# An attention layer in front of a mixture of experts: the softmax sums of a head move to two buffers, and three engines share the work on them differently

## The reference, cut to what matters

```
x = x + attention(layernorm(x))          # 1024 tokens, 384 channels, 12 heads of 32
t = x + moe(layernorm(x))                # 8 experts, top 2, hidden width 1536

attention, for each head:
  s   = (q * scale) @ k.T + rel_h + rel_w      # 1024 x 1024
  p   = softmax(s)                             # over the keys
  out = p @ v                                  # 1024 x 32
  then out @ w_proj + b_proj
```

## Time and profile before

| what | value |
|---|---|
| median of 3 runs | 608.98 us (608.33 to 609.45) |
| the profiled execution | 610.03 us, of which the span from first to last instruction is 608.2 us |
| TensorE busy | 584.4 us, 96% of the span |
| VectorE, ScalarE, GpSimd busy | 387.2, 297.9, 195.3 us |
| mean granted TensorE clock | 0.994 of full speed |
| attention, heads 0 to 11 | about 82 to 283 us of the span |
| experts | about 320 to 608 us |

### The profile page before, as it was taken

How to read it: one execution, slowest core, us unless ns; L and a number is a source line. 1 busy time by engine, 2 the same in 40 slices (tenths; PEclk the granted TensorE clock), 3 DMA queues, 4 the chain that set the end, 5 groups by cost and what they waited for, 6 DMA issues and landing times.

```text
span 608.2 us, 11363 instructions
## 1 busy us (share of the span) xinstructions
PE 584.4 (96%) x4409; PEld 504.5 (83%) x4409; DVE 387.2 (64%) x644; ACT 297.9 (49%) x411; POOL 195.3 (32%) x114
## 2 busy tenths in 40 slices
PE   2998999999999999999999999999999999999996
PEld 1886786667776667767987999999999999999994
DVE  6656777777777677732978974555476545377525
ACT  3555424555555555554546445444545454455523
POOL 0400048989888888898000000000000000000000
PEclk9999999999999999999979999999999999999999
DMA  9046045333334444103231534444442444442302
GB/s 272 9 87 130 3 107 110 78 72 68 66 66 87 86 87 87 41 2 105 79 117 57 178 128 139 137 150 149 155 157 80 156 156 156 156 156 85 111 1 103
DMA packets 37414, 63.39 MB, mean 104 GB/s; under 512 B 3864, under 2 KB 32894, under 8 KB 37246
## 3 DMA queue, kind: packets, MB, share of 16 engines
q1 hardware_dynamic: 37374, 62.83, 36.6%
HBM read 44.16 MB, written 1.57 MB: 75 GB/s over the span
## 4 chain that ended last, share of the span: by engine, by line
PE 90%; DVE 5%; ACT 2%; DMA 1%; issue 1%; SPq 1%; DVEq 0%
PE ps L782 21%; PE ps L798 21%; PE ps L557 14%; PE ps L566 9%; PE ps L466 8%; PE ps L544 7%; DVE rhalf L1146 2%; PE ps L716 1%; PE ps L496 1%; PE ps L451 1%; DMA onehot<-c_onehot 1%; PE ps L753 1%; PE ps L728 1%; PE ps L809 1%; PE ps L590 1%
## 5 line engine op out<-in xcount | busy, mean ns | idle before, releaser
L1146 DVE TENSOR_REDUCE rhalf<-ps 128x1 f32<-128x512 f32 x192 | 131.4, 691 | 33.5 <-PE ps L544 32.4
L400 POOL TENSOR_TENSOR acc<-acc,prob 128x1024 f32<-128x1024 f32 x58 | 139.7, 2408 | 9.3 <-ACT prob L938 4.6
L938 ACT ACTIVATE prob<-ps 128x1024 f32<-128x1024 f32 x96 | 98.1, 1028 | 80.5 <-PE ps L557 80.3
L557 PE MATMUL ps<-qst,kst 128*128 128x512 f32 x384 | 115.6, 397 | 0.9 <-ACT prob L938 0.9
L427 POOL CAST dpc<-dpt 120x1024 fp32r<-120x1024 f32 (+1 forms) x3 | 3.1, 1039 | 275.1 <-PE ps L818 216.6
L782 PE MATMUL ps<-xeh,wih 128*128 128x320 f32 x288 | 89.6, 311 | 1.0 <-ACT xeh L1002 1.0
L798 PE MATMUL ps<-hh,woh 128*128 128x320 f32 x288 | 89.2, 310 | 0.0
L798 PE MATMUL ps<-hh,wol 128*128 128x320 f32 x288 | 89.0, 309 | 0.0
L782 PE MATMUL ps<-xeh,wil 128*128 128x320 f32 x288 | 89.0, 309 | 0.0
L798 PE MATMUL ps<-hl,woh 128*128 128x320 f32 x288 | 89.0, 309 | 0.0
L782 PE MATMUL ps<-xel,wih 128*128 128x320 f32 x288 | 89.0, 309 | 0.0
(11 more groups left out here) (159 smaller groups left out, 876.1 us busy)
## 6 DMA issues: line engine op xcount, KB each, us to landing
raw_i<-in_L_ffn_wi SPq DMA_DIRECT2D x32, 576.0 KB, 5.1
raw_o<-in_L_ffn_wo SPq DMA_DIRECT2D x32, 576.0 KB, 4.1
xs<-in_x SPq DMA_DIRECT2D x8, 384.0 KB, 4.8
qst<-qh SPq DMA_DIRECT2D x12, 256.0 KB, 3.1
qst<-relh SPq DMA_DIRECT2D x12, 256.0 KB, 3.8
qst<-relw SPq DMA_DIRECT2D x12, 256.0 KB, 4.4
kst<-kp SPq DMA_DIRECT2D x12, 256.0 KB, 5.0
qst<-ql SPq DMA_DIRECT2D x12, 128.0 KB, 3.1
```

Of the source, the lines that this page charges most:

```text
L400: nc.gpsimd.tensor_tensor(acc[:, :], acc[:, :], prob[:, slot_of(j, t), :], ALU.add).then_inc(sum_add, 1)
L557: last = mm(bank(2 * (t % 2) + half), kst[b][:, part, t * P:(t + 1) * P], qst[b][:, part, half * BANK:(half + 1) * BANK], start=part == 0, ...
L938: run(prob[:, slot_of(j, t), :], ps[:, 2 * (t % 2) * BANK:2 * (t % 2 + 1) * BANK], ACT.Exp).then_inc(exp_done, 1)
L1146: ve.tensor_reduce(rhalf[:, p // 2, p % 2:p % 2 + 1], bank(4 + p % 2), AX_X, ALU.max).then_inc(max_red, 1)
```

## The change

- There are two buffers for the denominator. GpSimd adds tiles 0 to 5 into `acc` as before, and its last addition, of tile 6, writes the new buffer `total`. It waits there (and no longer at the first addition) until TensorE has read the head before. The first addition of a head waits only until GpSimd's own last addition of the head before is done.
- VectorE adds tile 7 to `total` (`add_last`), between pieces 5 and 6 of the next head's maxima. TensorE's product of ones with tile 7 is gone in heads 0 to 10, and its product with the sum now waits for VectorE (`acc_whole`). The last head stays as it was, but for the order of one wait.
- ScalarE copies the head's values into `vh`, after the exponential of tile 5 of the head before.
- VectorE's loop over heads becomes two heads written out and two passes of three heads.
- `bpj` and `tri` share the place of two `vh` buffers and are loaded after the last scores, ahead of the rows of `x`. GpSimd's bias addition and the router's count wait for both.

Core of the diff:

```
@@ gpsimd
-            def head_values(h, b):
-                wait(pool, pv_mm, PAIRS_T * (h - 2))
-                nc.gpsimd.tensor_copy(vh[b][:, :, :], vt[:, :, bass.ts(h, HD)]).then_inc(vh_ready, 1)
             def add_probs(h, j, added=ADDED):
                 pool.wait_ge(exp_done, NT * h + 2)
-                wait(pool, pv_mm, PAIRS_T * h)
+                wait(pool, sum_add, (ADDED - 1) * h)
                 nc.gpsimd.tensor_tensor(acc[:, :], prob[:, slot_of(j, 0), :], prob[:, slot_of(j, 1), :], ALU.add).then_inc(sum_add, 1)
                 for t in range(2, added):
                     pool.wait_ge(exp_done, NT * h + t + 1)
                     pool.wait_ge(sum_add, (ADDED - 1) * h + t - 1)
-                    nc.gpsimd.tensor_tensor(acc[:, :], acc[:, :], prob[:, slot_of(j, t), :], ALU.add).then_inc(sum_add, 1)
+                    if t == added - 1:
+                        wait(pool, pv_mm, PAIRS_T * h)
+                    nc.gpsimd.tensor_tensor((total if t == added - 1 else acc)[:, :], acc[:, :],
+                                            prob[:, slot_of(j, t), :], ALU.add).then_inc(sum_add, 1)
+            pool.wait_ge(late_in, 32)
             for t in range(NT):
                 pool.wait_ge(x_in[t // XT], 32)
@@ tensor, values
                 if i == PAIRS_T - 1:
-                    quarters(slice(Q4, 2 * Q4), ones[:, 0:HD], prob[:, slot_of(b, NT - 1), :], False, False)
-                    pe.wait_ge(sum_add, (ADDED - 1) * (h + 1) - (ADDED - LAST_ADDED) * h_last)
-                    last = quarters(slice(Q4, 2 * Q4), ones[:, 0:HD], acc[:, :], False, True)
+                    if not h_last:
+                        pe.wait_ge(acc_whole, h + 1)
+                    last = quarters(slice(Q4, 2 * Q4), ones[:, 0:HD], total[:, :], False, True)
@@ scalar
+            def head_values(h, b):
+                wait(act, pv_mm, PAIRS_T * (h - 2))
+                run(vh[b][:, :, :], vt[:, :, bass.ts(h, HD)], ACT.Copy).then_inc(vh_ready, 1)
+                    if t == 5:
+                        head_values(h + 1, (j + 1) % 3)
@@ vector
+            def add_last(h, j):
+                dve.wait_ge(sum_add, (ADDED - 1) * (h + 1))
+                dve.wait_ge(exp_done, NT * (h + 1))
+                ve.tensor_tensor(total[:, :], total[:, :], prob[:, slot_of(j, NT - 1), :], ALU.add).then_inc(acc_whole, 1)
+            def head(h, j, first=False, early=False, more=True):
                 for p in range(0 if first else NEXT, 2 * NT):
+                    if p == NEXT + 1 and not first:
+                        add_last(h - 1, (j + 2) % 3)
@@ sync
             sp.wait_ge(s_mm, 8 * NH)
+            sp.wait_ge(pv_mm, PAIRS_T * (NH - 1))
+            sp.dma_start(bpj[:, :], b_proj.partition_broadcast(P)).then_inc(late_in, 16)
+            sp.dma_start(tri[:, :], tri_c).then_inc(late_in, 16)
```

More of the change, by code:

```diff
@@ L76, in metaformer_layer @@
     wrt = new("wrt", [P, DC, E])
+    s0 = at[0]
     stats = new("stats", [P, NT, 6])
@@ L83, in metaformer_layer @@
     gsc = new("gsc", [PS, NT])
+    at[0] = max(at[0], s0 + 4 * P)
     base = at[0]
@@ L117, in metaformer_layer @@
     wph = place("wph", [P, DC, D], F32R, q0 + 8 * T)
-    o4 = room(4 * 2 * BANK)
+    o4 = room(4 * BANK + 4 * T)
+    total = place("total", [P, T], F32, o4 + 4 * BANK)
     osb = place("osb", [P, BANK], F32, o4)
+    l0 = at[0]
     vh = [new(f"vh{b}", [P, NT, HD]) for b in range(3)]
-    mneg = place("mneg", [NT, P], F32R, o4 + 7 * BANK)
+    tri, bpj = place("tri", [P, P], F32, l0), place("bpj", [P, D], F32, l0 + 4 * P)
+    mneg = place("mneg", [NT, P], F32R, s0)
     rl = new("rl", [P, 2, NT // 2])
@@ L161, in metaformer_layer @@
     lmax, lsum, lrec = (new(n, [P, NT]) for n in ("lmax", "lsum", "lrec"))
-    assert at[0] <= end and max(top, end) <= nc.sbuf_usable_end
+    assert at[0] <= end <= l0 and max(top, end) <= nc.sbuf_usable_end
     ctx = ExitStack()
@@ L932, in free_slot @@
                     wait(act, sum_add, (ADDED - 1) * then + max(1, was))
+                else:
+                    wait(act, acc_whole, then + 1)
             def exps(h, j, between):
@@ L948, in attn_high, with between, at_tile @@
                     run(ath[:, c, half * BANK:(half + 1) * BANK], bank(4 + half), ACT.Copy).then_inc(turn_act, 1)
-            exps(0, 0, lambda t: None)
+            def between(h, j):
+                def at_tile(t):
+                    if t == 1:
+                        copy_output(h - 1)
+                    if t == 5:
+                        head_values(h + 1, (j + 1) % 3)
+                return at_tile
+            act.wait_ge(v_dve, NT)
+            head_values(0, 0)
+            exps(0, 0, lambda t: head_values(1, 1) if t == 5 else None)
             with act.Fori(0, (NH - 3) // 3) as i:
                 for j in range(1, 4):
-                    exps(3 * i + j, j % 3, lambda t: copy_output(3 * i + j - 1) if t == 1 else None)
-            exps(NH - 2, (NH - 2) % 3, lambda t: copy_output(NH - 3) if t == 1 else None)
+                    exps(3 * i + j, j % 3, between(3 * i + j, j % 3))
+            exps(NH - 2, (NH - 2) % 3, between(NH - 2, (NH - 2) % 3))
             def last_between(t):
@@ L1168, in _ @@
             NEXT = 5
-            def head(h, first=False, early=False, more=True):
+            def add_last(h, j):
[3 more added lines that the diff above has]
+            def head(h, j, first=False, early=False, more=True):
                 for p in range(0 if first else NEXT, 2 * NT):
+                    if p == NEXT + 1 and not first:
+                        add_last(h - 1, (j + 2) % 3)
                     if p == 8 and not first and not early:
@@ L1193, in _ @@
                     negate_max(0)
-            head(0, first=True)
-            head(1, early=True)
-            with dve.Fori(2, NH - 2) as h:
-                head(h)
-            head(NH - 2, more=False)
+            head(0, 0, first=True)
+            head(1, 1, early=True)
+            head(2, 2)
+            head(3, 0)
+            with dve.Fori(0, (NH - 6) // 3) as i:
+                for j in range(4, 7):
+                    head(3 * i + j, j % 3)
+            head(NH - 2, (NH - 2) % 3, more=False)
+            add_last(NH - 2, (NH - 2) % 3)
             def attn_low(c):
```

17 lines of the change are left out of this document (8 added, 9 removed).

## The result

The changed kernel took 620.07 us, the median of 4 runs (617.78 to 628.21), against 608.65 us for the kernel before on the same chip (608.08 to 609.45). The ratio is 1.0168, with a 95% interval of 1.0145 to 1.0191. So the changed kernel is slower by about 10 to 11 us. The forecast was 622.3, in a range from 617 to 634. The profiled execution took 620.59 us, with a span of 618.3 against 608.2.

The account below looks back on a forecast made before the run. TensorE, busy 96% of the span, was the bound. Head 0 (+0.35), nine heads (7.1) and head 10 bring +9.8 on 608.98: 618.8; none to three lost races at 2.3 each put the middle at 622.3, range 617 to 634.

Parts of the forecast that it names:

- The ring: TensorE's denominator, tile 2's scores and exponential, GpSimd's five additions, VectorE's addition: no slack, 0.79 us more a head.
- P: Start of a head's timeline: TensorE's load of weights for piece 8, at 153.38 in head 4 before the change.
- The step to piece 8: On TensorE, from the load for the sum to the load for piece 8: 0.76 us, next P at P + 17.45.
- Head 10: GpSimd copies `wph` first (1.14 us), so VectorE starts 1.1 us later and adds 1.22; TensorE then at +9.8 us.
- The stall at piece 10: TensorE waits some 0.6 us at piece 10 for piece 8's late reduction; no cost by itself, but delays next tile 1.
- The race: VectorE's addition against GpSimd's next first one, both after GpSimd's last addition; margins about 0.05 us; none to three lost: 0.55.
- The price of a lost race: If GpSimd goes first, VectorE starts 2.3 us later and a head takes 19.8 us.
- GpSimd first in all ten heads: Rival: GpSimd beats VectorE in all ten heads, 642 us; four or more heads, 628 to 642, had chance 0.30.
- Who holds the port: VectorE and GpSimd share ports under an exclusive lock: whoever starts first runs whole; sharing would cost under 1.2 us a head.
- ScalarE's copies at nothing: ScalarE's copy of the values, put in 3.25 us of idle time ahead of tile 6: free, at most 1 us a head.
- The late transfers at nothing: Two more transfer issues and 256 KB ahead of the rows of `x`: hidden, some 2 us of cover at the tightest.
- queue behind the wait: Rival: reductions queued behind VectorE's wait make the next maximum row late, one more us a head, 629; chance 0.07.

Follow-up runs that it names:

- the kernel that lost seven: Changed kernel with VectorE's addition placed later, behind the reductions of pieces 5 to 7 and the division; VectorE was second in seven heads; 642.79 us.
- the kernel with half an addition: Changed kernel with VectorE adding only 512 of the 1024 columns of tile 7, the other half left out of the denominators; 622.74 us.

## Why the prediction was right, point by point

- *The ring.* Right, and shown from three sides: with VectorE's addition out all but 1.1 us of the cost is gone (610.05), with half of it the heads are 0.55 us shorter, and with tile 2's scores ahead of the wait TensorE no longer waits for `total`. The sizes were P + 15.33, 16.65 and 16.69 for event, sum and load; the trace has 15.38, 16.64 and 16.69 in a head written out, and 15.40, 16.75 and 16.80 in VectorE's loop, where its addition starts 0.12 us after the event and not 0.10.
- *The step to piece 8* was put at 0.76 us behind the load for `total` and took 0.60 in every head. With the later loads in the loop this makes 17.29 to 17.43 where 17.45 was forecast, 6.5 us over nine heads instead of 7.1.
- *Head 10*: 2.3 forecast, 2.04 measured. VectorE's addition there is recorded at 276.82 with 2.13 us, behind GpSimd's copy of `wph` (276.72, 1.15).
- *The stall at piece 10*: 0.6 forecast, 0.55 measured at 124.16 and up to 0.67 in the loop, and no cost by itself, as said: where it was taken away and VectorE still went first, heads took as long.
- *The race.* The margins were forecast at about 0.05 us; by the starts of the rows they are 0.00 to 0.01 in four heads of the loop and 0.04 to 0.24 in the others. The forecast's 622.3 counted one or two lost races. The profiled run lost none, and its time, 620.59, is the sum for none (610.03 and 9.8 are 619.8) and 0.8 more. So the middle of the forecast was high by its races, some 3.5 us, and its sum low by what came before the first scores (1.17 us) and by 0.4 for the table load, less what the heads and the end took less. Whether the run of 628.21 lost some can't be told, since it has no trace; its granted clock of 0.985 would fit, between the 0.995 of the profiled run and the 0.972 to 0.977 of the kernel that lost seven.
- *Luck.* The path and its lengths were right by their working, but that the time came within the range hung on four heads decided by 0.01 us or less. Had these been lost, at 2.2 us or more each, the time would have been about 629 or more (an estimate), and the forecast gave 628 to 642 a chance of 0.30.
- *The price of a lost race* at 2.3 us was right for the race alone and left the clock out. The single lost race in the kernel with half an addition cost 2.2 us (TensorE waited 2.63 us, and its clock stayed full), and the first one of the later-addition kernel 2.3 (19.54 against 17.28). Where TensorE's clock fell as well, such heads took 20.6 to 22.0, 3.2 to 4.6 us over 17.4. The rival "GpSimd first in all ten heads" was put at 642 and its kernel took 662.76; with seven lost it was 642.79.
- *Who holds the port.* The rows said that the two instructions run whole after one another, and every run since agrees: 3.42 for 2.40 on GpSimd, 3.38 for 1.22 on VectorE. That is the rule of the Trainium skill, "SBUF — State Buffer", section "SBUF: two separate sides"; sharing of bandwidth would have stretched both, and the winner is never stretched (1.23, 2.34).
- *ScalarE's copies at nothing.* The copies are free where they lie (0.41 us each), but the first one pulled the table load of 1.28 us behind it, ahead of the first exponential; before, it lay at 70.41 in 12 us of idle time. That costs less than 1.28, since TensorE goes on with pieces meanwhile: tile 2's exponential starts 4.86 us after the first scores before and 4.87 now, and only GpSimd's first sum ends 0.37 later. The Trainium skill, "ScalarE: Activation LUTs", section "What ACT_TABLE_LOAD costs", gives 1283 ns for the load and a drain of about 1380 more. The trace agrees with the load; no drain is in it, since the load starts 0.02 us behind the copy's end and the exponential 0.01 us behind the load's.
- *The late transfers at nothing.* Right: GpSimd waits 4.42 us for `x` and starts at 295.07, and the first residual is at 299.40, paced by TensorE (its wait is for `ps`).
- *The rival "queue behind the wait"* fell with the later addition: its intervals with VectorE first are 17.30 and 17.28 us, no shorter than before.

## What to carry to other kernels

Before work moves from the busiest engine to another, follow the result back to where that engine waits for it: if what the busiest engine issues behind the wait is what the helper chain starts from, the helper's time is paid in full in every pass, and the saving isn't seen at all. The cure is the order (issue the start of the next chain ahead of the wait), but a new order has a price of its own: here it cost some 0.7 us a head, half of it for a split group of products (0.35), against the 0.43 that the product saved. With the group whole again the time was that of the kernel before, and no version that computes all of it beat it. Where VectorE and GpSimd wait for the same event, make the order certain by a wait; here that came with a spread of 1.2 us in five runs, where four runs without it had 10, and the median stayed (619.93 and 620.07).

## What the runs showed of the hardware that was not expected

- TensorE's granted clock fell from 2.4 to 1.2 GHz (0.50 from 130 to 132 us with GpSimd first) around waits of 3.15 to 3.9 us in otherwise full heads, though not at one of 3.32 us (at 157.86 in the kernel with the later addition). Waits of 0.7 to 1.4 us left it at 1.00 over 192 us, and so did single ones of 2.33 and 2.63 us.
- VectorE starts 0.03 us after the semaphore it waits for in heads written out and 0.12 to 0.15 in its loop, GpSimd 0.08 after it, or 0.16 after ScalarE's exponential in its loop: whether a head stands in a loop can decide a race.
- One more group of 32-column products among the 128-column ones costs some 0.35 us a head; around such a group the weight loads pause 0.36 us ahead and 0.41 behind.
